# Relative-position values in blocks of two queries, and value products of two steps issued together

## What is computed

```python
dist = jnp.clip(idx[None, :] - idx[:, None], -R, R) + R
pe_k, pe_v = rel_emb_k[dist], rel_emb_v[dist]
...
score = jnp.einsum('bhqd,bhkd->bhqk', q, k) + jnp.einsum('bhqd,qkd->bhqk', q, pe_k)
attn = jax.nn.softmax(score, axis=-1)
ctx = jnp.einsum('bhqk,bhkd->bhqd', attn, v) + jnp.einsum('bhqk,qkd->bhqd', attn, pe_v)
```

## Time and profile before

| | us |
|---|---|
| median of three runs (2382.85 to 2384.37) | 2383.76 |
| profiled execution | 2382.3 |
| its span on the core | 2380.6 |
| PE busy in the span | 2282.5 |
| DVE busy | 1906.6 |
| ACT busy | 1429.9 |
| POOL busy | 600.4 |

### The profile page before, as it was taken

How to read it: one execution, slowest core, us unless ns; L and a number is a source line. 1 busy time by engine, 2 the same in 40 slices (tenths; PEclk the granted TensorE clock), 3 DMA queues, 4 the chain that set the end, 5 groups by cost and what they waited for, 6 DMA issues and landing times. The chain is left out here.

```text
span 2380.6 us, 49031 instructions
## 1 busy us (share of the span) xinstructions
PE 2282.5 (96%) x19244; PEld 1182.6 (50%) x19244; DVE 1906.6 (80%) x3711; ACT 1429.9 (60%) x2720; POOL 600.4 (25%) x355
## 2 busy tenths in 40 slices
PE   7989999999999999999999999999999997999997
PEld 3515544444444444444444454444444444666665
DVE  6777888888888888888888888888888725999996
ACT  3406666666666666666666666666666673444442
POOL 5502222323322222222222222232332220111111
PEclk9959999999999999999999999999999998999999
DMA  5733533332333343433332333333222221111110
GB/s 157 199 88 91 138 85 93 94 95 83 92 92 92 97 110 96 108 99 96 92 93 84 99 98 85 92 97 92 83 83 84 76 77 43 45 44 44 47 50 20
DMA packets 275667, 210.43 MB, mean 88 GB/s; under 512 B 17058, under 2 KB 266628, under 8 KB 275332
## 3 DMA queue, kind: packets, MB, share of 16 engines
q1 hardware_dynamic: 274308, 203.37, 30.9%
q0 software_dynamic: 1152, 4.19, 0.6%
HBM read 113.35 MB, written 93.34 MB: 87 GB/s over the span
## 5 line engine op out<-in xcount | busy, mean ns | idle before, releaser
L1118 DVE TENSOR_REDUCE amax<-psA 128x1 f32<-128x512 f32 x2048 | 1300.5, 683 | 274.2 <-PE psA L828 270.1
L1085 ACT ACTIVATE probs<-psS 128x512 f32<-128x512 f32 x1792 | 927.3, 610 | 378.9 <-PE psS L936 378.9
L828 PE MATMUL psA<-keys,queries 96*128 96x512 bf16 x2048 | 772.0, 390 | 3.1 <-DVE amax L1118 1.9
L936 PE MATMUL psS<-queries,keys 102*128 102x512 bf16 (+7 forms) x2176 | 604.2, 342 | 0.1
L850 PE MATMUL psC<-probs,vals 128*32 128x512 f32 (+7 forms) x4352 | 475.0, 524 | 0.5 <-ACT probs L1085 0.5
L786 POOL TENSOR_TENSOR band_probs<-band_probs,side 128x2048 f32<-128x2048 f32 x64 | 288.9, 4534 | 515.6 <-PE psC L948 515.6
L828 PEld LDWEIGHTS psA<-keys,queries 96*128 96x128 bf16 x2048 | 195.3, 97 | 319.8 <-DVE amax L1118 179.3
L936 PEld LDWEIGHTS psS<-queries,keys 102*128 102x128 bf16 (+1 forms) x2176 | 205.9, 98 | 184.4 <-ACT rel_scores L1064 29.9
L1080 ACT ACTIVATE band_probs<-psS 128x512 f32<-128x512 f32 x256 | 153.0, 598 | 152.2 <-PE psS L925 152.0
L850 PEld LDWEIGHTS psC<-probs,vals 128*32 128x32 f32 (+1 forms) x4352 | 89.1, 102 | 193.8 <-ACT probs L1085 137.5
L1442 PE MATMUL psG<-w_gate_up_T,f_xqT 128*128 128x352 f32 x512 | 160.4, 467 | 0.9 <-ACT f_xqT L1496 0.9
(11 more groups left out here) (161 smaller groups left out, 2014.3 us busy)
## 6 DMA issues: line engine op xcount, KB each, us to landing
rel_skew<-rel_scores SPq DMA_DIRECT2D x32, 2048.0 KB, 7.5
rel_near<-rel_skew SPq DMA_DIRECT2D x64, 1024.0 KB, 8.2
keys<-k_ring SPq DMA_DIRECT2D x48, 256.0 KB, 5.8
queries<-q_parts SPq DMA_DIRECT2D x192, 64.0 KB, 2.4
ctx_d<-rden SPq DMA_DIRECT2D x32, 256.0 KB, 2.3
ctx_in<-ctx_d SPq DMA_DIRECT2D x32, 256.0 KB, 2.7
q_parts<-parts SPq DMA_DIRECT2D x16, 384.0 KB, 3.0
k_ring<-parts SPq DMA_DIRECT2D x12, 384.0 KB, 3.3
```

The costliest lines, as they stand in the source:

```text
L828: t.matmul(small("M", m, n), qs[0:NR, qb, h, u * P:(u + 1) * P], keys[0:NR, par, h, c0:c0 + NQ], start=True, stop=True).then_inc(small_rea ...
L936: ins = t.matmul(bank[:, o:o + k], keys[0:nr, par, h, c0:c0 + P], qs[0:nr, qb, h, q0:q0 + k], start=True, stop=True, skip_group_check=True)
L1085: ins = a.activation(probs[:, n % 4, half], src, ACT.Exp)
L1118: v.reduce_max(amax[:, pair, k:k + 1], small("M", m, n), AX.X).then_inc(small_taken, 1)
```

## The change

Values are now taken for two steps at once: `VV` in steps 0, 4, 6, 8, 10, 12 and 14 holds the two steps before, and `probs` has buffers for three steps, with the value counter's head start raised from 2 to `PSTEPS` = 3. Positions work in blocks of 2 queries: one unit of 64 matmuls with 32-column slices, four of them over the four 32-partition parts of one whole `psA` bank, then one mask operation of 512 columns on VectorE and one fold of 16 matmuls. `mask_q` has 2 columns in place of 4, and `fold` 4 parts in place of 2. Relative products move from steps 4 to 7 to steps 0, 1, 4 and 6 (`RSTEPS`), and the relative maxima have a letter `X` of their own in the step after. The turn-back stands right behind the band values. `ORDER` is rewritten for all of this; it has 64 `M` as before. In the diff, what is left out are widths of tiles, arguments and the counter's offset that follow from these lines.

```diff
@@ -397,12 +397,12 @@
             def masks():
                 dve.wait_ge(k_ident, 1)
                 dve.wait_ge(k_masks, 3)
-                ch.link(v.tensor_add(c.mask_q[:], c.mask_v[:, 0:4], c.mask_v[:, 4:8]))
+                ch.link(v.tensor_reduce(c.mask_q[:], c.mask_v[:].rearrange("p (j q) -> p q j", q=2), AX.X, ALU.add))
                 ch.link(v.tensor_reduce(c.head[:], c.ident[:].rearrange("p (h c) -> p h c", h=HG)[:, :, 0:HD], AX.X, ALU.add))
                 ch.link(v.memset(c.fold[:], 0.0))
-                for half in range(2):
-                    rows = slice(64 * half, 64 * half + 64)
-                    ch.link(v.tensor_reduce(c.fold[rows, half, 0:HD], c.ident[rows].rearrange("p (g d) -> p d g", d=HD), AX.X, ALU.add))
+                for part in range(4):
+                    rows = slice(32 * part, 32 * part + 32)
+                    ch.link(v.tensor_reduce(c.fold[rows, part, 0:HD], c.ident[rows].rearrange("p (g d) -> p d g", d=HD), AX.X, ALU.add))
 
             moments(0)
             normalise(0)
@@ -540,21 +540,21 @@
 
 ROUND = APAIRS * APER
 
-RSTEP = 4
 RUNITS = APAIRS // 4
 SEQ = UNITS + RUNITS
-
-PSTEP = 8
+RSTEPS = (0, 1, 4, 6)
 
 ORDER = (
-    "SMSMVMSMSMMM", "SMSMMSMMSMMD", "SMSMVMMBSSM", "SMSSMSVM",
-    "SMSSMSMVRM", "SMSSMSVRM", "SMSSMSMVRM", "SMSSMSVRM",
-    "SMSSMSMVPM", "SMSSMSMVPM", "SMSSMSMVFPM", "SMSSMSMVPM",
-    "SMSSMSVFM", "SMSSMSVMT", "SMSSMSVM", "SMSSMSVM",
+    "SMSMMVVMSMMSMRMM", "SMSMSMXSMRMD", "SMSMMVBMXSS", "SMSSMSM",
+    "SMSMSMSMVVMR", "SSMXSS", "SMSMSMSMVVMR", "SSMXSS",
+    "SMSMSMSMVVPM", "SMSMSSM", "SMSMSMSMVVFMM", "SMSSMS",
+    "SMSMSMSMVVM", "SMSSMST", "SMSMSMSMVVM", "SMSMSSM",
 )
 RATE = tuple(x.count("M") for x in ORDER)
 ASTEPS = 13
 
+PSTEPS = 3
+
 WSTEPS = range(7, 13)
 
 SBANKS, ABANKS = 4, 3
@@ -564,12 +564,12 @@
 
 def place(n, ends=False):
 
-    return n if ends else n + min(max(n // 2 - RSTEP, 0), RUNITS)
+    return n if ends else n + sum(r < n // 2 for r in RSTEPS)
 
 
 def rel_place(k):
 
-    return 2 * (RSTEP + k) + 2 + k
+    return 2 * RSTEPS[k] + 2 + k
 
 
 def first_of(it):
@@ -656,9 +656,9 @@
         keys, qs, vals, keys_in, q_in = io.keys, io.qs, io.vals, io.keys_in, io.q_in
         rel = sb("rel_scores", [P, APAIRS, DREL])
         near = sb("rel_near", [P, APAIRS, 2, P])
-        probs = sb("probs", [P, 4, 2, NQ])
+        probs = sb("probs", [P, 2 * PSTEPS, 2, NQ])
         band = sb("band_probs", [P, 2, HG, CH, P])
-        relp = sb("rel_products", [P, 2, NQ])
+        relp = sb("rel_products", [P, NQ])
         amax = sb("amax", [P, APAIRS, APER])
         relm = sb("rel_max_of", [P, APAIRS])
         rcol = sb("rden_cols", [P, APAIRS])
@@ -949,36 +949,35 @@
                                          band[:, e, h, u, :], start=(u == 0 and e == 1), stop=False, skip_group_check=True)
                     ins.then_inc(band_read, 1)
 
-                def positions(k):
-
-                    slot_free("P", it, k)
-                    if k == 0:
-                        pe.wait_ge(band_mixed, it + 1)
-                    src = band[:, 0].rearrange("p h u (b q) -> p (h u) b q", q=4)
-                    for r in range(4):
-                        for side in range(2):
-                            block = 8 * k + 2 * r + side
-                            y = P - 4 - 4 * block
-                            ins = t.matmul(small("P", it, k)[64 * side:64 * side + 64, r * 64:(r + 1) * 64].rearrange("p (x q) -> p x q", q=4),
-                                           c.tv[:, y:y + 4, :].rearrange("p y d -> p (y d)"), src[:, :, block, :],
+                def positions():
+
+                    slot_free("P", it)
+                    pe.wait_ge(band_mixed, it + 1)
+                    src = band[:, 0].rearrange("p h u (b q) -> p (h u) b q", q=2)
+                    for r in range(16):
+                        for part in range(4):
+                            block = 4 * r + part
+                            y = P - 2 - 2 * block
+                            ins = t.matmul(small("P", it)[32 * part:32 * part + 32, r * 32:(r + 1) * 32].rearrange("p (x q) -> p x q", q=2),
+                                           c.tv[:, y:y + 2, :].rearrange("p y d -> p (y d)"), src[:, :, block, :],
                                            start=True, stop=True, skip_group_check=True)
                     ins.then_inc(small_ready, 1)
 
-                def fold_positions(cc):
-
-                    pe.wait_ge(small_taken, taken("P", it, 2 * cc + 1))
-                    for side in range(2):
+                def fold_positions():
+
+                    pe.wait_ge(small_taken, taken("P", it))
+                    for part in range(4):
                         for h in range(HG):
-                            src = relp[:, cc % 2, :].rearrange("p (h u r q) -> p h u r q", h=HG, u=CH, q=4)[:, h]
-                            out = psC[32 * h:32 * h + 32, :].rearrange("p (u c r s q) -> p u c r s q", u=CH, c=2, r=8, s=2)
-                            t.matmul(out[:, :, cc, :, side, :], c.fold[:, side, :], src, start=False, stop=False, skip_group_check=True)
+                            src = relp[:].rearrange("p (h u r q) -> p h u r q", h=HG, u=CH, q=2)[:, h]
+                            out = psC[32 * h:32 * h + 32, :].rearrange("p (u r s q) -> p u r s q", u=CH, r=16, s=4)
+                            t.matmul(out[:, :, :, part, :], c.fold[:, part, :], src, start=False, stop=False, skip_group_check=True)
 
 
                 for step in range(STEPS):
                     if step == ASTEPS:
                         start_ahead()
                     score = near_half if step < BAND_STEPS else far_half
-                    half = 0
+                    half, values = 0, 0
                     for kind in ORDER[step]:
                         if kind == "M":
                             some(1)
@@ -987,11 +986,11 @@
                             half += 1
                         elif kind == "R":
                             if not ends:
-                                rel_products(it + 1, qb1, step - RSTEP)
+                                rel_products(it + 1, qb1, RSTEPS.index(step))
                         elif kind == "P":
-                            positions(step - PSTEP)
+                            positions()
                         elif kind == "F":
-                            fold_positions((step - PSTEP) // 2 - 1)
+                            fold_positions()
                         elif kind == "D":
                             if not first:
                                 denominators(it - 1)
@@ -1001,19 +1000,21 @@
                         elif kind == "T":
                             if not ends:
                                 turn_maxima(it + 1)
-                        elif step == 0:
-                            if not first:
-                                far_values(gp, qp, STEPS - 1)
-                        elif step == 2:
+                        elif kind == "V" and step == 2:
                             band_values()
-                        else:
-                            far_values(g, qb, step - 1, ends)
+                        elif kind == "V":
+                            back, values = 2 - values, values + 1
+                            if step:
+                                far_values(g, qb, step - back, ends)
+                            elif not first:
+                                far_values(gp, qp, STEPS - back)
                 if ends:
-                    far_values(g, qb, STEPS - 1, ends)
+                    for back in (2, 1):
+                        far_values(g, qb, STEPS - back, ends)
                     denominators(it)
                     turn_back(it)
 
-            pe.sem_inc(pv_done, 2)
+            pe.sem_inc(pv_done, PSTEPS)
             pe.wait_ge(keys_in, KDMAS * 16)
             pe.wait_ge(q_in[0], 6 * 16)
             for k in range(RUNITS):
@@ -1082,10 +1083,10 @@
                             if n % 2 == 0 and half == 0:
 
                                 act.wait_ge(pv_done, it * VALUE_STEPS + n // 2 - BAND_STEPS + 1)
-                            ins = a.activation(probs[:, n % 4, half], src, ACT.Exp)
+                            ins = a.activation(probs[:, n % (2 * PSTEPS), half], src, ACT.Exp)
                         ins.then_inc(unit_done, 1)
-                    if n % 2 == 1 and RSTEP <= n // 2 < RSTEP + RUNITS and not ends:
-                        copy_rel(it + 1, n // 2 - RSTEP)
+                    if n % 2 == 1 and n // 2 in RSTEPS and not ends:
+                        copy_rel(it + 1, RSTEPS.index(n // 2))
                 if ends:
                     copy_context(it)
 
@@ -1152,13 +1153,12 @@
                 todo = [] if ends else [(it + 1, n) for n in range(AHEAD, ROUND)]
                 ahead = [] if last and qb >= QB - 2 else [(it + 2, n) for n in range(AHEAD)]
 
-                def mask_positions(k):
-                    ready("P", it, k)
```

(29 more changed lines are left out.)

## The result

| | us |
|---|---|
| changed kernel, median of four runs (2428.16 to 2432.64) | 2431.64 |
| before, median of four runs | 2383.48 |
| ratio, 95% interval | 1.0198 (1.0182 to 1.0214) |
| span of the profiled execution, before and after | 2380.6, 2430.9 |

The change makes the kernel slower by 48 us. I had forecast 14 more, with the right sign, and 2431.6 lies inside the range of 2358 to 2445; but the size is over three times mine.

The account below looks back on a forecast made before the run. TensorE's instruction order was taken as the bound; 3.05 us saved against 3.65 of new waits gave +0.6 in 27 iterations and -0.4 in five, +14 us in all: forecast 2397 us, range 2358 to 2445.

Parts of the forecast that it names:

- What bounds the kernel: TensorE, busy 96% of the span, runs instructions in written order; time from one block's start to the next counts.
- Parts 1 and 3: Per iteration: fewer changes of TensorE's form, 21.4 to 17.3 us plus positions; new waits for PSUM banks, 3.65 us more.
- positions without leaving: The positions' block on TensorE, 1.05 us, without the 0.11 us for leaving the 32-column form.
- Part 2: Positions as 128 records in 32 groups of four take 1.05 us per iteration, between 1.18 and 3.5.
- low end: Positions' time from columns, 0.88 us, with 0.009 on each group: 1.18 us.
- rival of a floor: Each small position matmul has a minimum time: positions take 3.5 us, 78 us more in all, 2475; chance 0.15.
- rival of the pair that pays twice: Leaving and entering the form is paid between a pair's two value products too: 45 us more, 2440; chance 0.06.
- rival of cheap bursts: VectorE and ScalarE enter bursts emptier; new waits 3.5 us per iteration instead of 4.65: 2366; chance 0.25.
- part 4: What moves past other queues: SP's skewed store and reload leave earlier, positions stay within 1 us of their place; no term.
- No term: Part 4's size: moved store, reload and positions add nothing to the forecast time.
- The signs: Chances for the whole kernel: faster 0.26, same 0.17, slower 0.57.

Follow-up runs that it names:

- late: Changed kernel with all positions moved to step 12 and the fold to step 14, out of the skewed store's time: 2408.22 us, ratio 1.0101.
- halves: Changed kernel with positions in two units of 32 matmuls, each with its own bank and mask, behind steps 8 and 10's pairs; fold in step 12: 2396.53 us.
- store_late: Changed kernel with TensorE's program untouched, but SP holds the skewed store back until the positions are done: 2425.52 us, ratio 1.0181.
- tuned2: `halves` with the same blocks in a second spread order, other places for key products and for pairs within their steps: 2295.26 us, ratio 0.9628.

## Why the prediction was right and wrong

**What bounds the kernel** held: TensorE's order and its waits.

**Parts 1 and 3** came out close, each by its own row:

| step of the prediction | forecast | measured |
|---|---|---|
| pair of values, alone / before positions | 1.85, 1.74 | 1.85, 1.73 |
| eighth score behind relative products | 3.57 | 3.57 |
| eighth key product behind turn-back | 4.45 | 4.46 |
| behind positions | 4.35 | 4.42 |
| behind fold | 4.06 | 4.24 |
| seventh behind step 12's pair | 3.51 | 3.64 |
| positions without leaving | 1.05 | 1.24 |
| parts 1 and 2, saved per iteration | 3.05 | 3.0 |
| new waits per iteration | 3.65 | 3.8 |
| ordinary iteration, more than before | +0.6 | +0.8 |

**Part 2** was sized 0.19 too low, 6 us over the whole, which other blocks of parts 1 and 2 gave back but for 0.05; it is above the 1.18 of its low end, far from the 3.5 of the other. A group of four takes 39 ns, not 33. The Trainium skill's floor of about 25 ns ("TensorE: Matmul & The Clock Gate", section "Wait — 56ns, not 53.3ns?") does not hold for these records: 128 of them go in 1.24 us, 9.7 ns each, when they stand four beside each other. Counted by the 64 matmuls of the kernel it is 19 ns, still below. So the rival of a floor fell. The rival of the pair that pays twice fell with the 1.73. The rival of cheap bursts fell: new waits per iteration were 3.8, a little more than I counted, not fewer.

**What failed is part 4**, in these words: "The last is one step earlier (6 for 7), so SP's skewed store and reload leave earlier", and "No term". The positions start 4.2 us after that store is issued, in the midst of its 8 us, and they take eight times as many records in one block as before (128 for 16). In place of "no term" the runs showed seven holes, 25 us.

My reading is that TensorE used up the instructions that it had, and that the fetch of the next 16 KB got through when the store was over. That the holes depend on the store and on the length of the block is shown by `late`, `halves` and `store_late`; that TensorE goes on 1.4 to 1.5 us after an instruction packet, seven times out of seven, is shown by the trace; how much TensorE holds of instructions, and that these packets are its own, is not. The six long iterations are 23 us above the ordinary ones in sum. `late` is 23 us faster too, but not by the same items: it also lacks the hole of the first iteration (2.7) and has its own four (5). I had asked of each moved step what data it waits for and what its engine does, and not how many instructions a block takes and whether the DMA engines are free to bring more.

The account of the 50.3 us in the span: ordinary slow-down in the loop 18 (my parts 1 to 3, forecast 14), the holes 25, the stretch ahead of the first band values 3, that behind the last ones 4. These last 7 had no term either, and their cause stays open. So of the 36 us that the forecast missed, 25 are the holes, 4 the sizes of parts 1 to 3, and 7 are open.

**The signs**: the chances gave 0.57 to slower, from a net of +0.6 per iteration between two terms of 3 and 3.65. That balance held to 0.2. That 2431.6 lies in the range is luck: the upper part of the range stood for slower positions and for pairs that pay twice, neither of which came, and no rival had a hole in it.

## What to carry to other kernels

A narrower packing of small matmuls can be a gain in columns and a loss in instructions: count the records that a block issues, and look at what the DMA engines do in that moment; two blocks of half the size took 1.47 us for 1.34 and had no hole. Fewer changes of form are worth little if the blocks between them become bursts longer than the banks that couple the engines; the same blocks, with the order spread so that few waits for banks are left, went from 0.6% slower than before to 4.6% faster. The mean busy shares (DVE 80%) said nothing about it; the walk from bank to bank, with pace and hand-over from a few rows, gave the start of each eighth product to 0.2 us.

## What the runs showed of the hardware

- TensorE stood for 2.7 to 4.1 us from start to start, seven times, with no wait that explains it, while or just after one transfer held the 16 DMA engines at a share of 1.0. In the widest, the next packet of the instruction queue was 16 KB and moved within 0.1 us of the store's end; in all seven work resumed 1.4 to 1.5 us after it had landed. Both kernels' pages give that queue 16 packets more after the change (143 and 159), for 2048 more matmul records and as many weight loads.
- Behind the hole of 3.9 us TensorE's granted clock was 0.50 for 5.7 us, and the iteration was 5.8 longer. The clock fell so behind four of the seven holes (of 4.1, 4.1, 2.9 and 2.7 us) and stayed at 1.00 behind the other three (3.2, 3.1 and 2.7).
- f32 matmuls of 32 columns, four beside each other into the four 32-partition parts of a bank, ran at 9.7 ns per record over 128 records; 64-column ones, two beside each other, took 32 (0.51 us for 16).
- VectorE operations on SBUF of 0.28 to 0.52 us took 0.85 to 1.82 us where they started beside GpSimd's mix, and ended 0.15 to 0.4 us behind it (`tuned2`, 16 times).
- Moving one DMA behind a wait moves all that is queued behind it: in `store_late` TensorE waits 16.7 us for the shift rows where it waited 3.6, none of it at the transfer that was moved.
